# A fused attention and routed-FFN kernel on one Trainium2 core: the engine that issues the weight fetches

## What is computed

```python
x = x + xattn(layernorm(x), ctx, ctx, Wq, Wk, Wv, Wo)      # x, ctx: (16, 256, 256)
xf = layernorm(x)
top1 = argmax(softmax(xf @ gate_w.T))                      # two routed experts
masked = xf[None] * one_hot(top1).T[:, :, None]
h = relu(einsum('end,edh->enh', masked, w1) + b1[:, None]) # 256 -> 1024
routing = (einsum('enh,ehd->end', h, w2) + b2[:, None]).sum(0)
shared = relu(xf @ sw1 + sb1) @ sw2 + sb2
out = x + routing + shared
```

## Time and profile before

| | |
|---|---|
| median of 3 runs | 1181.67 us (1177.52 to 1187.94) |
| the profiled execution | 1187.45 us |
| its span in the trace | 1185.6 us |
| mean granted TensorE clock in it | 0.882 |
| PE busy | 77% of the span |
| DVE, POOL, ACT busy | 58%, 42%, 38% |
| weights fetched into WR | 64 transfers of 1024 KB, 9.2 us to landing (median) |

### The profile page before, as it was taken

How to read it: one execution, slowest core, us unless ns; L and a number is a source line. 1 busy time by engine, 2 the same in 40 slices (tenths; PEclk the granted TensorE clock), 3 DMA queues, 4 the chain that set the end, 5 groups by cost and what they waited for, 6 DMA issues and landing times. The chain is left out here.

```text
span 1185.6 us, 21905 instructions
## 1 busy us (share of the span) xinstructions
PE 916.6 (77%) x7526; PEld 751.4 (63%) x7526; DVE 688.6 (58%) x1168; ACT 447.2 (38%) x974; POOL 492.3 (42%) x816
## 2 busy tenths in 40 slices
PE   2466868778798788878797788878798888879754
PEld 2334656766677577767676576756677576758654
DVE  4677664646666664646576664646576674736110
ACT  3231614334343434334344434334343434334322
POOL 6323414243534435243534335243534335345733
PEclk7576969989899998989899888989898988979877
DMA  8566555556282746556282736656281736450750
GB/s 222 144 206 136 163 84 214 81 178 125 79 191 50 224 58 221 80 187 114 88 183 76 202 54 221 80 194 107 92 185 52 223 52 220 62 187 11 292 188 9
DMA packets 95456, 164.03 MB, mean 138 GB/s; under 512 B 9008, under 2 KB 81456, under 8 KB 86720
## 3 DMA queue, kind: packets, MB, share of 16 engines
q1 hardware_dynamic: 75264, 69.16, 31.0%
q10 hardware_dynamic: 9792, 71.31, 15.2%
q0 software_dynamic: 10368, 23.14, 7.3%
HBM read 123.66 MB, written 39.91 MB: 138 GB/s over the span
## 5 line engine op out<-in xcount | busy, mean ns | idle before, releaser
L1241 POOL TENSOR_TENSOR hl<-h,hh 128x256 fp32r<-128x256 f32 x264 | 193.2, 742 | 459.9 <-ACT hh L782 459.5
L970 DVE RECIPROCAL T<-nd 128x256 f32<-128x256 f32 x128 | 224.6, 1755 | 176.1 <-PE nd L490 164.1
L964 DVE TENSOR_REDUCE nmax<-work 128x8 f32<-128x512 f32 x256 | 162.1, 679 | 79.6 <-PE work L460 79.6
L761 ACT ACTIVATE PT<-work 128x512 f32<-128x512 f32 x256 | 137.9, 602 | 140.4 <-PE work L475 99.1
L460 PE MATMUL work<-KP,QP 96*128 96x512 f32 x256 | 105.8, 487 | 76.4 <-DMA QP<-scratch_q 46.2
L475 PE MATMUL work<-QP,KP 128*128 128x256 f32 x512 | 93.1, 307 | 68.1 <-ACT PT L761 64.8
L475 PEld LDWEIGHTS work<-QP,KP 128*128 128x128 f32 x512 | 74.6, 202 | 87.7 <-ACT PT L761 81.2
L420 PE MATMUL hid<-XS,WS 128*128 128x256 f32 x816 | 128.3, 313 | 0.0
L420 PEld LDWEIGHTS hid<-XS,WS 128*128 128x128 f32 x816 | 116.0, 215 | 7.6 <-issue 7.6
L460 PEld LDWEIGHTS work<-KP,QP 96*128 96x128 f32 x256 | 49.2, 209 | 110.5 <-DVE nmax L964 52.9
L782 ACT ACTIVATE h<-hid,bias 128x256 f32<-128x256 f32 x144 | 68.5, 475 | 121.5 <-PE hid L420 112.8
(11 more groups left out here) (186 smaller groups left out, 1506.0 us busy)
## 6 DMA issues: line engine op xcount, KB each, us to landing
WR<-wx ACTq DMA_DIRECT2D x64, 1024.0 KB, 9.2
KP<-scratch_k SPq DMA_DIRECT2D x96, 128.0 KB, 5.0
QP<-scratch_q SPq DMA_DIRECT2D x96, 128.0 KB, 8.6
scratch_k<-T SPq DMA_DIRECT2D x16, 512.0 KB, 3.0
scratch_q<-T SPq DMA_DIRECT2D x16, 512.0 KB, 3.2
wx<-WR POOLq DMA_DIRECT2D x16, 512.0 KB, 3.7
stages<-wraw POOLq DMA_DIRECT2D x24, 256.0 KB, 5.2
rowin<-queue SPq DMA_DIRECT2D x16, 260.0 KB, 9.1
```

Source lines behind the costliest of these rows:

```text
L761: nc.scalar.activation(PT[:, j % 4].rearrange("p t q -> p (t q)"), work[:, BANK[("st", j)], :], ACT.Exp).then_inc(sem["exp_done"], 1)
L964: nc.vector.tensor_reduce(nmax[:, t, 8 * p:8 * p + 8], work[:, BANK[("s", j)], :].rearrange("q (b k) -> q b k", k=BLOCK), AX_X, ALU.max, n ...
L970: nc.vector.reciprocal(T[:, p, :], nd[:, p % 2, 1, :]).then_inc(sem["inverted"], 1)
L1241: nc.gpsimd.tensor_tensor(R(hl[:, k % 2, a]), h32[:, k % 2, a], hh[:, k % 2, a], ALU.subtract).then_inc(sem["hl_done"], 1)
```

## The change

`load_weights` leaves ACT's list and joins SP's. On SP it stands behind `spread` and ahead of `load_ctx`, `load_x` and `store`. The body is the same, with one constant wait exchanged. For i = 15, where no spread is issued, it stands behind `load_residual`; for i = 16 behind `load_tile(16)`. Two other sets of fetches for the left tokens (`load_left_weights`) stay on ACT.

```diff
@@ sync engine @@
+            def load_weights(i):
+
+                selected, = held(sp, sp_counts, i - 1)
+                sp.wait_ge(sem["ident_loaded"], 16)
+                sp.wait_ge(sem["sel_done"], selected)
+                if type(i) is int and i == 2:
+                    sp.wait_ge(sem["wx_stored"], 16 * (PIECES - SHARED_PIECES))
+                expert = sp.value_load(control[0:1, 1:2], min_val=0, max_val=1)
+                for k in range(RU):
+                    if type(i) is not int or i > 2:
+                        sp.wait_ge(sem["w2_done"], unit_no(i, k) + 1)
+                    sp.dma_start(WR[:, k].rearrange("p a b c -> p (a b c)"),
+                                  wx[bass.ds(expert * P, P), k].rearrange("p a b c -> p (a b c)")) \
+                        .then_inc(sem[f"wr_loaded{k}"], 16)
+
             def iteration(i, more, loads=True):
...
                     spread(16 * (i + 1), "q_bounced", "k_bounced")
+                if type(i) is not int or i >= 2:
+                    load_weights(i)
                 if more and loads:
                     load_ctx(i + 2)
                     load_x(i + 2)
...
             load_tile(LAST + 1)
+            load_weights(LAST + 1)
             store(LAST + 1)
@@ scalar engine @@
-            act_counts = [act.alloc_register("act_count")]
-
-            def load_weights(i):
...
                 relu(i, 5)
-                if type(i) is not int or i >= 2:
-                    load_weights(i)
                 if type(i) is int and i == 0:
                     act.wait_ge(sem["proj_lo"], 4)
                 exps(i, 0)
...
             relu(i, 4)
-            load_weights(i)
             relu(i, 5)
```

## The result

| | before | after |
|---|---|---|
| median of 4 runs each | 1182.58 us | 1251.81 us |
| lowest to highest | 1177.52 to 1187.94 | 1249.17 to 1255.88 |
| profiled execution's span | 1185.6 us | 1249.6 us |
| mean granted clock | 0.882 | 0.859 |

The changed kernel is slower by 5.9%: the ratio is 1.0588, with a 95% interval of 1.0532 to 1.0643, or 69 us between the medians. The forecast was 1271 us in a range of 1233 to 1306.

The account below looks back on a forecast made before the run. No engine full; PE's recurring waits for an exponential and the spread count. Per iteration +11.0 - 2.9 - 1.0 = +7.1, times 13, less 3 for iteration 15: +89 us, so 1271 us for the median, range 1233 to 1306.

Parts of the forecast that it names:

- The wait for unit 0: PE in front of `up(0, i+1)`: stands from s + 6.8 to s + 18.0, 11.2 us in place of none.
- SP gets the fetches, behind the spread: SP's ring, worked off in order: unit 0 lands one unit's time behind the spread, at s + 18.0.
- my lower bound of 2.7: Pace of one weight unit on SP's ring: taken as 3.0 us, bounds 2.7 and 3.6.
- The half clock behind it: PE after the wait for unit 0: 4 us at half clock, costing 2.0 us more before the first score product.
- ACT's gain: ACT between relu and first exponential: idle time before the exponential goes, -2.94 us per iteration, passed whole to PE.
- The clock behind the stall: PE after its wait for the exponential: the slow stretch mostly goes, -1.0 us per iteration, between 0 and 2.
- The moved context: Context of two sequences on, behind four units on SP: lands at s + 27.7, costs 0 to 0.5 us, taken as 0.
- The fast one: Rival at SP's ring: weights pass beside the spread, unit 0 lands at s + 11.7; 1170 us, chance 0.04.
- My point against this rival: SP's ring: the context moved over all partitions and still landed behind the spread.
- The milder one: Rival at SP's ring: weights fill gaps of the spread, half clock costs 1 us; +50, 1232 us, chance 0.16.
- The heavier one: Rival: with 3.6 us per unit, the late context also holds ACT and score products; +123, 1305 us, chance 0.20.
- the rule of 512 bytes: Smallest transfer for full line rate; by it the spread's 1.5 MB would be through in about 4 us.

Follow-up runs that it names:

- `weights_behind_context`: Against the changed kernel, the four fetches on SP moved behind the context and x of two sequences on: 1276.96 us, ratio 1.0772.
- unit 0 ahead: Against the changed kernel, unit 0 fetched ahead of the spread on SP, units 1 to 3 left behind it: 1187.83 us, ratio 1.0026.
- small weights: Changed kernel, but in iterations 3 to 15 each unit moves 64 bytes per partition in place of 8 KB: 1231.42 us, ratio 1.0366.
- the four extra transfers: Changed kernel plus four 128 KB transfers between spread and weights, each to 16 partitions: 1307.06 us, ratio 1.1044; its pair, to 128 partitions: 1269.50 us.

## Why the prediction was right, and where its sizes were off

*The wait for unit 0.* The step "SP gets the fetches, behind the spread" held as put. The spread lands at s + 15.0, as forecast. Unit 0 lands at s + 17.5 where I had 18.0, and PE starts 0.2 us later, at 17.7. So a unit takes 2.5 us behind the spread, below my lower bound of 2.7, and the other three follow it 2.5 us apart. That is 1 MB at 417 GB/s, not at the 360 that I took from a stretch with other transfers in it; the earlier trace rows had 410 in another stretch, which is 2.6 us per unit, so my bound of 2.7 and my sentence that 1 MB had never done better were both misread from the rows.

*The half clock behind it.* From `up(0)` to the first score it is 25.60 - 17.70 = 7.90 us; I had 6.0 + 2.0, right in its sum. The half clock lasts longer than the 4 us that I took: in iteration 8 PE works at 0.50 for the 5.65 us from its start to 661.

*ACT's gain.* 2.97 us against 2.94. Two other runs, which keep the fetches away from the exponential in other ways and let nobody wait for weights, have the same 0.36 us between relu and exponential and end 67 and 71 us below the kernel before.

*The clock behind the stall.* This is the term that was too small. I took -1.0 within 0 to -2; it is -1.53. The turns themselves show that it is the clock. The stretch from first exponential to s holds the same products each time and goes by the clock granted in it, here twice in the kernel before and once in the changed one (us, PE, PEld, DVE, ACT and POOL busy, clock, DMA share, GB/s):

```profile
524.20:544.20 20.00, 19.34 (x178) 14.04 (x178) 12.62 (x12) 9.82 (x20) 6.24 (x11) 0.83 0.62 229
590.80:609.80 19.00, 18.22 (x178) 13.40 (x182) 12.67 (x12) 9.87 (x20) 7.21 (x12) 0.91 0.68 249
619.80:637.20 17.40, 16.68 (x178) 12.24 (x182) 12.63 (x12) 9.82 (x21) 9.27 (x14) 1.00 0.29 63
```

Half clock takes up 4.8 us of this stretch on the mean before the change and 0.8 behind it. The other 0.51 us came from the stretch between first score and last relu, which I had at no change. Before, the wait for the spread ended in the score products, and the clock's fall came behind it; now the wait and the slow stretch lie ahead of them. The half clock in this stretch goes from 6.6 to 5.5 us; with the fetches ahead of SP's wait, where the wait for the spread stays in the score products, it is 6.6 and the stretch 28.6 us, near the 28.75 of before. That this part of the gain is the clock is read off its course; no run changes the clock alone.

*The sum.* 13 x 10.65 = 138 us of loss and 13 x (2.97 + 1.53 + 0.51) = 65 us of gain. From the first score of iteration 15 to the end the changed kernel is 7.0 us shorter, and up to the first score of iteration 2, where no fetch has been moved yet, 2.4 us. In all +64 us, which is the difference of the two traces' spans, 1249.6 - 1185.6. The 69 between the medians lies 5 us above it, no more than what single executions of the kernel before differ by (1177.52 to 1187.94; the profiled one took 1187.45). The forecast had 13 x 7.1 - 3 = 89. Of the 25 us too much against the traces, 13 x 0.35 = 5 are the landing of unit 0 and what follows it, 13 x (0.53 + 0.51) = 14 the clock, 4 that iteration 15 and the tail give back 7 us and not 3, and 2 lie ahead of the change.

*The moved context.* Taken at 0, and it is: `weights_behind_context` lands it 10 us earlier and the stage behind it is as long as ever. It lands at s + 25.8 and not at 27.7, since a unit takes 2.5 us and not 3.0; that is 0.3 us behind the first score, and ACT, which reads it in iteration 8 only 1.4 us behind that score, no longer waits for it. The cover is the late score. Where the score comes nearly in time, as with unit 0 ahead, the context holds ACT for 11 us, of which PE loses about 0.5.

*The rivals.* The fast one had the weights pass the spread. In one ring they do not (small weights still wait). On a ring of their own they do, and the run that did so was the slowest but one, because the spread then pays. My point against this rival was the context's landing; the full answer is that the DMA engines had no room to give. The milder one had unit 0 land 1 us behind the spread: it was 2.5. The heavier one needed 3.6 us per unit, where it was 2.5, and 2 us for the late context.

*The rule that I weighed.* I set the rule of 512 bytes in the Trainium skill, "DMA: Bandwidth & Descriptors", section Specifications, against the spread's 117 GB/s and said that the trace does not agree. The runs show that the length of the row was not the matter: the same rows of 1 KB take 0.37 us per 128 KB on 128 partitions, which is 354 GB/s, and 0.96 us on 16. Another rule bears on this, the one in the Trainium skill, "SBUF — State Buffer", section "Door 1: The DMA port swizzle (why `[64,N]` ≈ `[32,N]`)": the bandwidth depends on how many of the 16 ports the partitions reach, four partitions in a row sharing one. By that rule 16 partitions reach 4 ports, a quarter of the 436 GB/s that the skill's page gives for all 16, which makes an estimate of 109 GB/s. The trace agrees roughly: 117 in the spread and 137 in the four extra transfers, both somewhat above it. In both, transfers in a row go to different groups of 16 partitions; whether that makes the difference no run here shows. My fast rival had the partitions as its "reason of its own" and concluded that the weights would pass beside the spread at their own rate; in the run on two rings the sum of both was 308 GB/s, where the weights alone run at 417.

## What to carry to other kernels

A queue that issues transfers is an ordered list twice over: the engine waits in it, and the ring behind it is worked off in the same order. When a fetch is moved, ask what stands ahead of it in the new ring and how long that takes to drain, not to issue; here 5.6 us of issuing were 15.0 us of draining. And take the gain apart from the place: what ACT needed was that nothing stands between relu and exponential, which a move by two instructions, or to another queue's early part, gives for nothing (1121 and 1117 us against 1188 for the kernel before on the same chip).

## What the runs showed of the hardware that I had not expected

- A second ring gave no more room here. Weights in rows of 8 KB to 128 partitions and a spread in rows of 1 KB to 16, on two rings: the weights were little disturbed (10.8 us to landing against 9.2, both medians), the queries of the spread took 19.3 us in place of 8.6. Whether the larger rows or the spread's few partitions decide who yields is not shown.
- In that run SP itself was held in issuing: the context's issue took 3.72 us and the next one's 4.43, where both take 0.4 in the kernel before. It needs no second ring: with the weights ahead of the spread in SP's own, the six issues of the queries took 5.71 us in its iteration 8, where they take 2.8 in the kernel before.

```profile
664.43 3.72 SPq L280 DMA_DIRECT2D ctx_in<-ctxT  x1
668.25 4.43 SPq L269 DMA_DIRECT2D xin<-x  x1
```

- ACT's queue runs ahead of the engine: it issues fetches while earlier activations are still in work, 0.10 us behind the start of the first exponential in the run with the fetches behind two of them. So here a fetch in ACT's list held only what stood behind it, and only where the engine had no work in hand.
